# Layer 0 of a graph network stack: the pad term written to one lane of the sum, the other lanes cleared by a transfer

## The reference, cut to what matters

```python
h = jnp.maximum(_layernorm(x, axis=-1), 0.0)
mask = (adj > 0.0)
xj_proj = h @ W1a
diff = h[:, :, None, :] - h[:, None, :, :]
z = relu(xj_proj[:, :, None, :] + diff @ W1b + b1)     # 192 channels
hm = jnp.einsum('bjkh,bjk->bjh', z, mask)
x = x + hm @ W2 + deg[..., None] * b2
```

## Time and profile before

| | |
|---|---|
| median of 3 runs | 1465.24 us (1464.78 to 1468.52) |
| the profiled execution's own time | 1462.28 us |
| its span, first to last instruction | 1460.6 us |
| mean granted TensorE clock | 0.969 |
| busy: PE, PEld | 1320.8 us (90%), 1073.9 us (74%) |
| busy: DVE, ACT, POOL | 1176.9 us (81%), 1108.5 us (76%), 498.5 us (34%) |
| moved by DMA | 18.11 MB in 40925 packets, mean 12 GB/s |

### The profile page before, as it was taken

One profiled execution on the slowest core, in us unless ns is written; L12 is line 12 of the kernel. 1 busy time (PEld: TensorE's weight loads), 2 busy tenths in 40 slices (PEclk: granted clock), 3 DMA queues, 4 the chain that ended last, 5 costly groups with the idle time before them and its releaser, 6 DMA issues. The chain is left out here.

```text
span 1460.6 us, 41314 instructions
## 1 busy us (share of the span) xinstructions
PE 1320.8 (90%) x11243; PEld 1073.9 (74%) x11244; DVE 1176.9 (81%) x3034; ACT 1108.5 (76%) x2426; POOL 498.5 (34%) x611
## 2 busy tenths in 40 slices
PE   3999999999999999999999999997999997972398
PEld 1777778777787777777778777775889887910398
DVE  7899998999999998999989999984444445978755
ACT  4788888888888888888888888873555555916676
POOL 1343344443334444434344443332222111066400
PEclk9999999999999999999999999998999998986599
DMA  7000000000000000000000000000000000000022
GB/s 153 23 10 9 7 8 14 7 7 7 7 14 7 7 7 8 13 7 7 7 14 7 7 7 7 0 2 1 1 0 0 0 0 0 0 1 0 4 54 57
DMA packets 40925, 18.11 MB, mean 12 GB/s; under 512 B 19572, under 2 KB 40886, under 8 KB 40886
## 3 DMA queue, kind: packets, MB, share of 16 engines
q1 hardware_dynamic: 40354, 17.42, 4.9%
q10 hardware_dynamic: 532, 0.21, 0.1%
HBM read 13.44 MB, written 4.19 MB: 12 GB/s over the span
## 5 line engine op out<-in xcount | busy, mean ns | idle before, releaser
L725 DVE SCALAR_TENSOR_TENSOR acc<-slot_banks,acc 128x768 f32<-128x768 f32 x512 | 487.2, 952 | 58.2 <-PE slot_banks L441 50.8
L794 POOL TENSOR_TENSOR acc<-acc 128x384 f32<-128x384 f32 x128 | 128.2, 1001 | 551.1 <-DVE onediff L719 543.6
L441 PE MATMUL slot_banks<-ac_hi,work 128*128 128x192 f16 x1408 | 264.9, 247 | 12.1 <-DVE work L707 10.2
L441 PE MATMUL slot_banks<-ac_lo,work 128*128 128x192 f16 x1408 | 263.8, 246 | 0.0
L441 PEld LDWEIGHTS slot_banks<-ac_hi,work 128*128 (+1 forms) x1408 | 137.1, 97 | 79.1 <-issue 58.6
L441 PE MATMUL slot_banks<-ac_hi,onediff 128*128 128x192 f16 x1024 | 183.1, 246 | 2.7
L441 PE MATMUL slot_banks<-ac_lo,onediff 128*128 128x192 f16 x1024 | 182.2, 246 | 0.0
L441 PEld LDWEIGHTS slot_banks<-ac_lo,work 128*128 (+1 forms) x1408 | 138.0, 98 | 22.7 <-issue 16.9
L541 ACT ACTIVATE work<-bank 128x512 f16<-128x512 f32 x256 | 130.7, 601 | 1.2 <-PE bank L352 1.2
L780 POOL TENSOR_TENSOR ac_lo<-ac,ac_hi 128x384 f16<-128x384 f32 x128 | 118.8, 929 | 32.4 <-ACT ac_hi L581 32.4
L707 DVE TENSOR_SCALAR work<-work,slot_key 128x1024 f16 x256 | 117.6, 479 | 9.5 <-issue 1.0
(11 more groups left out here) (260 smaller groups left out, 3303.3 us busy)
## 6 DMA issues: line engine op xcount, KB each, us to landing
adj_in<-in_adj_dram SPq DMA_DIRECT2D x32, 256.0 KB, 2.8
out_dram<-acc SPq DMA_DIRECT2D x32, 128.0 KB, 2.0
l1w<-in_L_gnn_W_dram SPq DMA_DIRECT2D x2, 64.0 KB
l1b<-in_L_gnn_b_dram SPq DMA_DIRECT2D x2, 64.0 KB
x_all<-in_x_dram SPq DMA_DIRECT2D x4, 0.2 KB, 11.7
nm_in<-in_nodemask_dram ACTq DMA_DIRECT2D x1, 64.0 KB
w1a<-in_L_gnn_W_dram ACTq DMA_DIRECT2D x1, 48.0 KB
w1b<-in_L_gnn_W_dram ACTq DMA_DIRECT2D x1, 48.0 KB
```

The costliest lines, as they stand in the source:

```text
L441: last = nc.tensor.matmul(unit(pair, t, 1), hot(t), part[:, q, H:2 * H].unsqueeze(1), start=False, stop=(e == 1 and (t % SB == SB - 1 or t ...
L725: nc.vector.scalar_tensor_tensor(out=sums, in0=unit((q + k) % 2, 0, SU), scalar=0.0, in1=sums, op0=ALU.min, op1=ALU.add).then_inc(s_free[k ...
L794: nc.gpsimd.tensor_tensor(acc[:, q, 0:2 * H], acc[:, q, 0:2 * H], acc[:, q, 2 * H:4 * H], ALU.add)
```

## The change

ScalarE writes the whole pad term to lane 0 (192 columns) in place of a quarter of it to each of four lanes (768 columns). `neg_pad` isn't divided by four any more. Lanes 1 to 3 (576 columns) of each graph's sum are set to zero by a transfer within SBUF, from a new tile `zeros` of 192 columns that is read three times over; GpSimd fills that tile once as its first instruction. SyncE's queue issues the transfers: those for the first three graphs behind the weight loads, and from then on one in each step, for graph b+3 once graph b-1 (which has the same place q) is transposed. `act_pads` waits for the transfer's semaphore instead of for `s_hm` (the sum of the graph four before is complete). The loads of adjacency move into the same stepwise program of SyncE, in the step of the first graph of a group.

```diff
+        zeros = place(2 * H).bitcast(F32)
...
             act.wait_ge(s_n, g + 1)
             act.wait_ge(s_hi, b + 1)
-            if not (known(b) and b < 4):
-                act.wait_ge(s_hm, b - 3)
-            nc.scalar.activation(acc[:, q, :].rearrange("p (t h) -> p t h", t=SU),
-                                 ac32[:, q, 0:H].unsqueeze(1).broadcast_to([N, SU, H]), ACT.Relu,
+            act.wait_ge(s_clear[q], 16 * g + 16)
+            nc.scalar.activation(acc[:, q, 0:H], ac32[:, q, 0:H], ACT.Relu,
                                  scale=neg_pad[:, p, q:q + 1]).then_inc(s_acc0, 1)
...
-            v.tensor_scalar(neg_pad[:, p, :], pad[:, :], -float(SS - 1), 1.0 / SU, ALU.add, ALU.mult).then_inc(s_n, 1)
+            v.tensor_scalar(neg_pad[:, p, :], pad[:, :], -float(SS - 1), None, ALU.add).then_inc(s_n, 1)
...
-                with sp.Fori(1, NI) as i:
-                    for p in range(2):
-                        sp.wait_ge(s_adjTp, 2 * i + p - 1)
-                        load_adj(sp, 2 * i + p, p)
+                def clear_lanes(q):
+
+                    sp.dma_start(acc[:, q, H:SU * H].rearrange("p (t h) -> p t h", t=SU - 1),
+                                 zeros.unsqueeze(1).broadcast_to([N, SU - 1, H])).then_inc(s_clear[q], 16)
+
+                def step(b, g, u, q, nxt, p, use):
+                    if q == 0 and not (known(g) and g + 2 >= NG):
+                        sp.wait_ge(s_adjTp, g + 1)
+                        load_adj(sp, g + 2, u)
+                    if not (known(b) and b + 4 > B):
+                        if not (known(b) and b < 1):
+                            sp.wait_ge(s_T, b)
+                        clear_lanes((q + 3) % GS)
+
+                sp.wait_ge(s_zeros, 1)
+                for q in range(GS - 1):
+                    clear_lanes(q)
+                all_iterations(sp, step)
+                for q in range(GS):
+                    sp.wait_ge(s_clear[q], 16 * NG)
...
             def _(pool):
                 g = nc.gpsimd
+                g.memset(zeros, 0.0).then_inc(s_zeros, 1)
```

More of the change, by code:

```diff
@@ L308, in gnn_stack_kernel @@
         s_acc0 = sem("sum_initialised")
+        s_zeros = sem("zeros_made")
+        s_clear = [sem(f"sum_lanes_cleared{q}") for q in range(GS)]
         s_G = sem("onehot_chunk_made")
```

## The result

The changed kernel has a median of 1476.93 us (1474.54 to 1479.36, 5 runs) against 1465.24 us (1462.70 to 1468.52, 5 runs) for the kernel before: a ratio of 1.0081, interval 1.0065 to 1.0097. It is 0.8% slower, 11.7 us. The forecast was 1466.2 us, no change, with a range up to 1470.

The account below looks back on a forecast made before the run. PE and DVE handing slot banks to each other were taken to bound the kernel. 1462.28 + 0.5 (start) + 0.5 (traffic) + 0 (pads) = 1463.3 us profiled; the median lies 2.96 above, so 1466.2 us, range 1462 to 1470.

Parts of the forecast that it names:

- Traffic beside the engines: Layer 0: 38 MB more written into SBUF might slow DVE's 512 sums; 0.5 us, between 0 and 2.0.
- The rival: DVE's sums and PE's reads beside SBUF-to-SBUF clears: traffic slows them, 24.5 us at 5% a sum, 1491; chance 0.06.
- Shorter pads: ACT's L589, 768 to 192 columns: 0.49 us less each, worth 0 on the path; upper bound 63 us.
- ACT's busy time: Sign to look for: ACT busy about 63 us less, from 128 pads shorter by 0.49 us.
- the idle time before L598: Sign to look for: ACT's idle ahead of L598 grows by nearly the 63 us taken off its busy time.
- The rival by which ACT's relief reaches the ring: Steady part: lighter ACT takes the seed off PE's path in one graph of four, 15.7 us, 1450.5; chance 0.05.
- the ring: Layer 0's steady part: PE and DVE hand the slot banks to each other in turn, setting 7.5 us a graph.
- The clears' landing: Steady part: clears land in about 3 us against 11.6 us of cover before the pads; price 0 on the path.
- The start: Before graph 0: GpSimd's memset (0.15 to 0.3 us) and pads late behind the first clear; together 0.5 us, bounds 0.1 and 1.7.
- the rival of the earlier trace: Last graph of a group, L699 beside POOL's L780: 0.69 us collisions moved on or off, 22 us; chance 0.02 each way.
- Collisions in the steady part: GpSimd and VectorE colliding more or less at L699: 1488 or 1444, chance 0.02 each.
- Engines beside transfers: The skill's rule that engine and DMA ports are disjoint: by it the traffic term would be 0, the sum 0.5 us less.

Follow-up runs that it names:

- e2: Changed kernel with only the first clear of each of the four places, short pads kept: 1465.64 us, ratio 1.0015, steady part 953.8 us.
- the early read alone: Kernel before, with PE's sequencer reading the next graph's count late in the step before: 1458.92 us, ratio 0.9954; again 1457.69 us, ratio 0.9936.
- both: Changed kernel with PE's count read a step earlier and the first three clears ahead of the weight loads: 1454.88 us, ratio 0.9922; again 1454.63 us, ratio 0.9920.

## Why the prediction was wrong, point by point

**The step that failed is "Traffic beside the engines"**, with 0.5 us, between 0 and 2.0. Its measured size is 8.8 us, and what the runs showed in its place is a slower read by PE's sequencer: 0.61 us in place of 0.30, on the path once in four graphs. The term went wrong in two places. I priced the clears by what they do to DVE's vector work, and there they do nothing that shows (the sums' mean is 952 ns in both kernels), but PE's sequencer reads SBUF for itself, 128 times, and this read was in none of my rows. And the transfers beside which I read prices all came from HBM. The rival named that difference ("both ends are in SBUF") and still looked for its effect on sums and matmuls, priced at 1491. Its sign was right, and its mechanism was not: the sums were no slower.

**What I could have read.** The row "issue: 8.0, 16" ahead of L434 showed that in half of the first graphs of groups PE already waited for its sequencer. There was a step, then, in which a delay of the sequencer can count in full. In the trace of before, the packets of an adjacency load start 1.0 us behind its issue, and the reads for the first graph of a group lie 1.2 or 1.7 us behind the transposes that were to set off the clears. With that the price could not have been known, but a bound could: as an estimate, a read delayed by the 1.0 us or more that such a load's packets take, 32 times, is 32 us or more. The term's range ended at 2.0.

**Shorter pads, 0.** Right. L591 takes 0.45 us (0.44 forecast), and e2 shows the steady part unchanged to 0.1 us. ACT's busy time fell by 48 us and not by 63: the 128 pads themselves take 61.5 us less (119.4 to 57.9), but ACT's instructions overlap in the trace (L583 runs from 39.35 for 0.49 us, L584 from 39.73), and such overlap counts once. Nor did the idle time before L598 grow by nearly that, but by 28 us; another 14 went to ACT's wait for the transposes, ahead of L611 (4.0 to 18.5 us). The rival by which ACT's relief reaches the ring is refuted for this kernel.

**The clears' landing, 0.** Right in the steady part: they land 2.6 us after issue (median of 128), against the 11.6 us of cover that were forecast, with no wait of ACT. SP's issue takes 0.59 us instead of 0.4; no wait in the trace points at it.

**The start, 0.5 us.** It measured 1.6, inside its bounds of 0.1 and 1.7. The pads ended at 39.25 us, just behind the 38.5 to 39.1 forecast, as the clear landed 3.4 us after its issue instead of 3.2. The memset's share did not show: DVE's start-up row ended 0.26 us earlier than before. What I had not followed is what a DVE that is a microsecond late runs into: L720 beside L781, 0.59 us. That is the kind of collision which the rival of the earlier trace rows priced for the steady part, here once, at the start, and between other instructions.

**Collisions in the steady part.** Neither on nor off: three kinds of step are within 0.4 us in all, and the mean of L699 (L700 after) is 514 ns before and 512 after. The rule of the Trainium skill on them (SBUF — State Buffer, "Who interferes with whom") agrees with L720, a VectorE instruction with two inputs in SBUF that went from 0.69 to 1.28 us when a GpSimd instruction that reads SBUF had started before it.

**Engines beside transfers.** The Trainium skill (SBUF — State Buffer, "SBUF: two separate sides") says that engines and transfers can't slow each other, and that contention on the transfers' side arises where several DMA engines or remote cores write to it. I had read it as covering all that an engine does. For the vector work the runs agree; PE's read of a count out of SBUF they show going from 0.30 to as much as 0.76 us beside a transfer that reads SBUF. The measurement decides. The Trainium skill (Runtime: NRT & Kernel Launch, "Instruction fetch mechanics") describes the register loads that the runtime makes from HBM as round trips over AXI. If a loop's read of SBUF goes that way too, beside the transfers and not through the engine's ports, the two would fit. That is a guess: no run here shows which way the read goes.

**The sum with measured terms**: 1462.28 + 1.6 (start) + 8.8 (reads) = 1472.7 us for the profiled execution, and 4.0 more for the longer time behind layer 0 gives 1476.7, the 1476.71 measured. In the medians, 1465.24 + 10.4 = 1475.6 stands against 1476.93; the 1.3 us between them lie within the scatter of either kernel's runs.

## What to carry to other kernels

A sequencer that reads a loop count out of SBUF can have a place on the path like any matmul: look for "issue" ahead of the first work of a loop, however small, and try reading the count one round earlier. When a transfer is added, ask of it not only whether it lands in time, but what lies at the moment of its packets in each kind of step, the sequencers' reads included, and whether the rows that price it read and write the same memories. Where one kind of step out of four takes all of a loss, look for what only that step does, and move one thing in time before taking it away.

## What the runs showed of the hardware

A sequencer's read of one value out of SBUF took 0.28 to 0.32 us alone; only the first one of each sequencer took 0.49 to 0.55, in the kernel before too. Beside a transfer that reads SBUF it took 0.61 us on average for PE, 0.42 to 0.76 in single cases, and up to 0.79 for POOL, whether the transfer wrote to SBUF or to HBM; DVE's first read took 0.98 us beside the first three clears, where it took 0.55 in the kernel before. Beside a transfer from HBM into SBUF at 342 GB/s a read took 0.31. A further read with its check cost PE 0.70 us where nothing hid it, and moving the read that is there away gave back 0.27.

A read whose value nothing used did not stand in the trace, so an added cost has to be looked up there before its time is believed.

The stretch at 1.2 GHz behind layer 0 began when PE had been nearly idle, and its length differed between executions of the same kernel: 20.5 and 17.1 us in two of the early read alone, 10.2 and 13.7 in two of both, while the steady parts of each pair agreed within 0.3 us. What sets the length stays open.
